# Second batch's scatters spread over heads and logits, joint end chunks, and the token copies moved to ScalarE

## The reference

```python
scores = einsum('bhqd,bhkd->bhqk', q, k) * scale
sparsity = scores.max(-1) - scores.mean(-1)
_, top_idx = top_k(sparsity, U)                      # U = 307 of 2048
out_sel = softmax(q_sel @ k.T * scale) @ v
out = zeros_like(q).at[bi, hi, top_idx].set(out_sel) # a scatter
x = x + ga * (out @ Wo + bo)
logits = einsum('bnd,esd->bnes', xn, sn)             # token x slot
dispatch, combine = softmax(logits, over tokens), softmax(logits, over slots)
slots = einsum('bnd,bnes->besd', xn, dispatch)
eo = gelu(slots @ w1 + b1) @ w2 + b2
x = x + gb * einsum('bmd,bnm->bnd', eo, combine)
```

## Time and profile before

| what | us |
|---|---|
| three timed runs | 1577.94, 1582.79, 1583.1 |
| their median | 1582.79 |
| time of the profiled execution | 1569.39 |
| its span, first to last instruction | 1567.7 |
| attention of batch 0, PE busy from 456 to 580 | 117.70 of 124 |
| attention of batch 1, PE busy from 928 to 1040 | 108.13 of 112 |
| logits of batch 0, PE busy from 1043 to 1100 | 57.00 of 57 |

### The profile page before, as it was taken

The page is one execution under the profiler, slowest core; times in us unless marked ns, Lnnn a source line. Parts: engine busy times, 40 slices in busy tenths (PEclk is TensorE's granted clock), DMA queues, the critical chain, the costliest instruction groups (busy, mean ns, idle before and its releaser), DMA issues.

```text
span 1567.7 us, 28302 instructions
## 1 busy us (share of the span) xinstructions
PE 1457.8 (93%) x8701; PEld 804.4 (51%) x8706; DVE 1203.5 (77%) x2777; ACT 1034.4 (66%) x1420; POOL 270.5 (17%) x331
## 2 busy tenths in 40 slices
PE   7999999998889989999999889999999999999999
PEld 3542222223434432222222644444889986489988
DVE  5679999999887759999999888877855534775411
ACT  4578888887767878888888448863433463343453
POOL 1540000000720042111111214441111000011100
PEclk9999999999999999999999899999999999999999
DMA  5861111112432301111112212220143202024410
GB/s 178 266 170 40 40 40 40 42 44 85 152 106 72 79 12 46 50 48 43 42 42 82 68 38 64 55 75 16 62 162 134 91 33 75 0 85 149 139 48 33
DMA packets 94323, 119.40 MB, mean 76 GB/s; under 512 B 23726, under 2 KB 79630, under 8 KB 93724
## 3 DMA queue, kind: packets, MB, share of 16 engines
q1 hardware_dynamic: 91164, 117.66, 24.8%
q0 software_dynamic: 3072, 0.66, 0.3%
HBM read 93.46 MB, written 24.79 MB: 75 GB/s over the span
## 4 chain that ended last, share of the span: by engine, by line
PE 50%; DVE 34%; issue 11%; DMA 3%; ACT 2%; POOL 1%; SPq 0%; DVEq 0%; ACTq 0%
DVE work_area L1309 26%; PE psum L2156 7%; PE psum L2097 7%; PE psum L2220 7%; PE psum L2016 5%; PE psum L2007 4%; PE psum L2167 4%; PE psum L1988 3%; DVE big_area L1309 3%; PE psum L2176 3%; DMA work_area<-heads_out 2%; PE psum L2210 2%; PE psum L1809 2%; PE psum L1834 1%; DVE work_area L1380 1%
## 5 line engine op out<-in xcount | busy, mean ns | idle before, releaser
L1309 DVE CUSTOM_DVE_ANT_0 work_area<-psum,work_area 128x1024 f32<-128x1024 f32 x512 | 589.1, 1220 | 8.1 <-PE psum L1870 4.3
L902 ACT ACTIVATE work_area<-psum 128x1024 f32<-128x1024 f32 x512 | 510.4, 1027 | 76.2 <-DVE big_area L1309 32.3
L1870 PE MATMUL psum<-work_area 96*128 96x512 bf16 x1024 | 309.4, 384 | 47.9 <-DVE big_area L1309 6.8
L1860 PE MATMUL psum<-work_area 96*128 96x512 bf16 x1024 | 305.4, 380 | 7.4 <-ACT work_area L902 1.6
L1870 PEld LDWEIGHTS psum<-work_area 96*128 96x128 bf16 x1024 | 63.4, 97 | 266.4 <-DVE big_area L1309 251.2
L1860 PEld LDWEIGHTS psum<-work_area 96*128 96x128 bf16 x1024 | 88.7, 98 | 153.0 <-ACT work_area L902 59.0
L924 ACT ACTIVATE work_area<-psum 128x614 f32<-128x614 f32 x160 | 102.3, 682 | 29.8 <-PE psum L2007 28.7
L2156 PE MATMUL psum<-work_area,xn 128*128 128x128 f32 x1024 | 117.4, 275 | 0.5 <-ACT work_area L1008 0.5
L2156 PEld LDWEIGHTS psum<-work_area,xn 128*128 128x128 f32 x1024 | 115.8, 192 | 0.9 <-ACT work_area L1008 0.7
L2220 PE MATMUL psum<-expert_out,work_area 128*128 128x256 f32 x512 | 115.5, 379 | 0.0
L2097 PE MATMUL psum<-slots_T,work_area 128*128 128x512 f32 x256 | 115.0, 592 | 0.0
(11 more groups left out here) (267 smaller groups left out, 2080.4 us busy)
## 6 DMA issues: line engine op xcount, KB each, us to landing
work_area<-in_L_ffn_w_dram SPq DMA_DIRECT2D x32, 1024.0 KB, 5.3
work_area<-k_parts SPq DMA_DIRECT2D x192, 64.2 KB, 2.1
work_area<-q_parts SPq DMA_DIRECT2D x192, 64.0 KB, 2.1
k_parts<-work_area SPq DMA_DIRECT2D x24, 384.0 KB, 3.5
q_parts<-work_area SPq DMA_DIRECT2D x16, 384.0 KB, 2.7
big_area<-q_parts SPq DMA_DIRECT2D x16, 384.0 KB, 5.5
work_area<-k_parts SPq DMA_DIRECT2D x32, 192.0 KB
x_res<-in_L_attn_x_dram SPq DMA_DIRECT2D x8, 512.0 KB, 6.6
```

What stands on the lines that cost most here:

```text
L902: s.activation(SC[:, t % 4], PS[:, 2 * (n % 2):2 * (n % 2) + 2].rearrange("p a n -> p (a n)"), ACT.Relu).then_inc(relu_done, 1)
L1309: v.tensor_tensor_reduce(SC[:, t % 4], PS[:, 4 + 2 * (t % 2):6 + 2 * (t % 2)].rearrange("p a n -> p (a n)"), SC[:, t % 4], 1.0, -3.0e38, A ...
L1860: last = mm(PS[:, 2 * (n % 2) + k], QS1[par][0:TERMS, t * P:(t + 1) * P], KS[par][0:TERMS, k * 512:(k + 1) * 512], start=True, stop=True)
L1870: last = mm(PS[:, 4 + 2 * (t % 2) + k], QS1[par][0:TERMS, t * P:(t + 1) * P], KS[par][0:TERMS, K1 + k * 512:K1 + (k + 1) * 512], start=Tru ...
```

## The change

- `heads_out[b]` gets 16 rows more, one for each head, that nobody reads. The matrix of selected queries `QS` gets 13 more columns, set once for each batch by POOL, whose row number is such a spare row (plus the head).
- The last chunk of an even head stands in partitions 0 to 63 and that of an odd head in partitions 64 to 127 (`chunk_at`), and both share one buffer entry (`ON_ends`, `IDX_ends`), so two heads take 5 scatters and not 6: 40 for a batch. DVE writes each head's rows and places with two instructions each where there was one.
- Both batches keep rows and places of all heads in the space of the first weights. DVE's wait for scatters in `indices` goes; one wait for all scatters of batch 0 stands before the attention of batch 1. SP's and ACT's waits for all scatters before the weights and the slot maxima go too.
- Batch 0's scatters: one in every 6 maxima instead of 5. Batch 1's: the first 26 wait for a number of exponentials, 4.5 apart; the other 14 wait for one turned token tile each of batch 0's logits. `first_rows(1)` still waits for all of them.
- `keep_tokens` moves from POOL to ACT, behind each `turned`.

```diff
-    heads_out = [nc.dram_tensor(f"heads_out{b}", [L * H, DH], F32).ap() for b in range(B)]
+    heads_out = [nc.dram_tensor(f"heads_out{b}", [L * H + H, DH], F32).ap() for b in range(B)]
+    UW = 320
+    chunk_at = lambda j, par: j * P - (HALF_ROWS if j == CH - 1 and par else 0)
+    SCATTERS = (2 * PAIRS, 3 * PAIRS)
+    CHUNKS = [(h, j) for h in range(H) for j in range(CH - 1 + h % 2)]
+    IN_HEADS = 26
...
             def first_rows(b):
                 for k in range(2):
-                    sp.wait_ge(scattered[k], (b + 1) * PAIRS * CH * 16)
+                    sp.wait_ge(scattered[k], (b + 1) * SCATTERS[k] * 16)
...
             def weights(b):
                 sp.wait_ge(oT_used, B * H)
-                for k in range(2):
-                    sp.wait_ge(scattered[k], B * PAIRS * CH * 16)
...
+                for par in range(2):
+                    g.memset(QS[:, par, U:UW], float(L * H // 2))
...
+            def scatter_behind_heads():
+
+                for n, (h, j) in enumerate(CHUNKS):
+                    pool.wait_ge(on_ready, H + h + 1)
+                    if n < IN_HEADS:
+                        pool.wait_ge(p_ready, 2 + 128 + 13 + n * 9 // 2)
+                    else:
+                        pool.wait_ge(xt_ready, n - IN_HEADS + 1)
+                    scatter_one(1, h, j)
...
+                def keep_tokens(i, par, n):
+                    t = i * 2 + n
+                    s.activation(XN[:, t] if isinstance(t, int) else row(XN, t), XS[:, par], ACT.Identity).then_inc(xn_ready, 1)
+
                 if b:
                     turned(b, 0, 0, 0)
+                keep_tokens(0, 0, 0)
                 with act.Fori(0, NT // 2 - 1) as i:
                     for par in range(2):
                         turned(b, i, 1 - par, par + 1)
+                        keep_tokens(i, 1 - par, par + 1)
                         keep_logits(i, par)
...
+                    half = slice(par * HALF_ROWS, (par + 1) * HALF_ROWS)
                     dve.wait_ge(idx_ready, b * H + i * 2 + (n + 1))
-                    if b:
-                        dve.wait_ge(scattered[par], b * (PAIRS * CH * 16) + (i * (CH * 16) + (n // 2) * CH * 16))
-                    v.tensor_scalar(IDX[:, par] if b else of_head(IDX0, i, n), PS[:, 7, CH * P:CH * P + CH], hcol[:, bass.ds(i * 2 + n, 1)], None, ALU.add).then_inc(idx_used, 1)
+                    v.tensor_scalar(of_head(IDX, i, n), PS[:, 7, CH * P:CH * P + CH - 1], hcol[:, bass.ds(i * 2 + n, 1)], None, ALU.add)
+                    v.tensor_scalar(IDX_ends[half, bass.ds(i + n // 2, 1)], PS[half, 7, CH * P + CH - 1:CH * P + CH], hcol[half, bass.ds(i * 2 + n, 1)], None, ALU.add).then_inc(idx_used, 1)
...
-                    v.tensor_tensor(ON[:, par] if b else of_head(ON0, i, n), OR[:, :, 0:DH], ORr.rearrange("p (j o) -> p j o", o=1).to_broadcast([P, CH, DH]), ALU.mult).then_inc(on_ready, 1)
+                    half = slice(par * HALF_ROWS, (par + 1) * HALF_ROWS)
+                    v.tensor_tensor(of_head(ON, i, n), OR[:, 0:CH - 1, 0:DH], ORr[:, 0:CH - 1].rearrange("p (j o) -> p j o", o=1).to_broadcast([P, CH - 1, DH]), ALU.mult)
+                    v.tensor_scalar(ON_ends[half, bass.ds(i + n // 2, 1)].rearrange("p o d -> p (o d)"), OR[half, CH - 1, 0:DH], ORr[half, CH - 1:CH], None, ALU.mult).then_inc(on_ready, 1)
...
+                    for k in range(2):
+                        dve.wait_ge(scattered[k], SCATTERS[k] * 16)
                     spread(0)
```

More of the change, by code:

```diff
@@ L151, in adaln_block @@
         a = Area(Wqk[:].rearrange("p k c n -> p (k c n)"))
-        ON0 = a.take([H, CH, DH])
-        IDX0 = a.take([H, CH], U32)
+        ON = a.take([H, CH - 1, DH])
+        IDX = a.take([H, CH - 1], U32)
+        ON_ends = a.take([PAIRS, DH])
+        IDX_ends = a.take([PAIRS], U32)
         WoG = sb("Wo_gated", [P, DC, D])
@@ L227, in adaln_block @@
         OS = a.take([CH * P])
-        QS = a.take([2, UP], BF16)
+        QS = a.take([2, UW], BF16)
         PX = [a.take([2, UP]) for _ in range(2)]
@@ L235, in adaln_block @@
         ORr = a.take([CH])
-        ON = a.take([2, CH, DH])
-        IDX = a.take([2, CH], U32)
         PX_last = [a.take([2, UP]) for _ in range(2)]
@@ L374, in adaln_block @@
         rowv = lambda v: v.rearrange("(a d) -> a d", a=1).to_broadcast([P, D])
-        heads_rows = [h.rearrange("(t p h) d -> t p (h d)", p=P, h=H) for h in heads_out]
+        heads_rows = [h[0:L * H].rearrange("(t p h) d -> t p (h d)", p=P, h=H) for h in heads_out]
         @block.sync
@@ L426, in zero_rows @@
                 for b in range(B):
[L427 removed]
+                    hz = heads_out[b][0:L * H].rearrange("(p j) d -> p (j d)", p=P)
                     for k in range(2):
@@ L734, in attend, with scatter_chunk @@
[L734 to L752, removed]
+            def scatter_chunk(b, h, j):
+                g.indirect_dma_start(
+                    out=heads_out[b], out_offset=bass.IndirectOffsetOnAxis(ap=IDX[:, h, j:j + 1], axis=0),
+                    in_=ON[:, h, j], in_offset=None).then_inc(scattered[h % 2], 16)
@@ L754, in scatter_in_search, with scatter_ends, scatter_one @@
+            def scatter_ends(b, i):
+                g.indirect_dma_start(
+                    out=heads_out[b], out_offset=bass.IndirectOffsetOnAxis(ap=IDX_ends[:, i:i + 1], axis=0),
+                    in_=ON_ends[:, i], in_offset=None).then_inc(scattered[1], 16)
+            def scatter_one(b, h, j):
+                if j < CH - 1:
+                    scatter_chunk(b, h, j)
+                else:
+                    scatter_ends(b, h // 2)
             def scatter_in_search():
                 pool.wait_ge(zero_out, 64)
[L757 to L763, removed]
+                for n, (h, j) in enumerate(CHUNKS):
+                    pool.wait_ge(max_done, H * NT + 4 + (n + 1) * 6)
+                    scatter_one(0, h, j)
@@ L765, in experts @@
+            def scatter_behind_heads():
+                for n, (h, j) in enumerate(CHUNKS):
+                    pool.wait_ge(on_ready, H + h + 1)
+                    if n < IN_HEADS:
+                        pool.wait_ge(p_ready, 2 + 128 + 13 + n * 9 // 2)
+                    else:
+                        pool.wait_ge(xt_ready, n - IN_HEADS + 1)
+                    scatter_one(1, h, j)
             def experts(b):
-                with pool.Fori(1 - b, NT // 2) as i:
-                    for par in range(2):
-                        keep_tokens(b, i, par)
@@ L814, in _ @@
             pads(1)
-            attend(1)
+            scatter_behind_heads()
             experts(0)
@@ L1000, in slot_maxima @@
                     s.activation(MXR[:, at:end], PS[:, 6:8].rearrange("p a n -> p (a n)")[:, at:end], ACT.Identity).then_inc(mxr_ready, 1)
-                for k in range(2):
-                    act.wait_ge(scattered[k], B * PAIRS * CH * 16)
                 slot_maxima(0, 0, S)
@@ L2022, in rows @@
                     for j in range(CH):
-                        w = min(P, U - j * P)
-                        last = mm(PS[0:w, 7, CH * P + j:CH * P + j + 1], QS[0:TERMS + 5, n % 2, j * P:j * P + w], idx_rows[0:TERMS + 5, 0:1], start=True, stop=True)
+                        at = chunk_at(j, n % 2)
+                        w = min(P, UW - at)
+                        last = mm(PS[0:w, 7, CH * P + j:CH * P + j + 1], QS[0:TERMS + 5, n % 2, at:at + w], idx_rows[0:TERMS + 5, 0:1], start=True, stop=True)
                     last.then_inc(idx_ready, 1)
@@ L2030, in turn @@
                     for j in range(CH):
-                        last = tr(PS[:, 7, j * P:(j + 1) * P], OS[:, j * P:(j + 1) * P], identF[:])
+                        last = tr(PS[:, 7, j * P:(j + 1) * P], OS[:, chunk_at(j, n % 2):chunk_at(j, n % 2) + P], identF[:])
                     last.then_inc(oT_ready, 1)
```

6 lines of the change are left out of this document (1 added, 5 removed).

## The result

| | us, median (range, runs) |
|---|---|
| before, the same session | 1582.47 (1577.94 to 1583.41, 6) |
| after | 1571.88 (1568.75 to 1573.85, 6) |
| ratio | 0.9936, 95% interval 0.9923 to 0.9948 |
| profiled execution, before and after | 1569.39 and 1569.73 |

The changed kernel is 10.6 us faster in timed runs, while the two profiled executions differ by 0.3 us. Forecast was 1582.0 (1574 to 1590), no change. So the trace shown of the kernel before is that of an execution that did not lose the 10 us, and the experiments had to find one that did.

A forecast was written before the change was run, and what follows sets the result against it. The prediction took PE, busy 93% of the span, as the bound. All terms were worth 0 except -0.1 us from the long head, giving 1582.7 for the median of runs; it said 1582, range 1574 to 1590.

The forecast's parts named there:

- Three scatters a head cost a head nothing: In the attentions: heads 7.06 us apart with scatters and without, so scatters do not lengthen a head.
- Scatters of batch 1 out of the attention: Moving batch 1's scatters out of the second attention: worth 0 by the two equal head lengths.
- third rival: In timed runs, 13 us longer than profiled: spreading bursts of scatters gives up to 6.5 us, 1576; chance 0.11.
- The long head: One head of 8.11 us in the second attention: its whole surplus of 1.05 us bounds the gain, 0.1 taken.
- The two DVE instructions: Two more small DVE instructions a head, both attentions: 0.35 us a head, hidden behind DVE's waits, worth 0.
- first rival: In the attentions, DVE's additions reach PE: at most 11.2 us more, 1594; chance 0.09.
- The copies: Token copies on ACT in the logits: 0.42 us each, 1.9 us of ACT's wait remain, worth 0.
- The rows: Batch 1's first rows: issued from 1090.7, landing 1092.9 to 1096.3, before PE asks at 1097.69; worth 0.
- second rival: Batch 1's rows come late after the last scatters: PE waits 0.95 us, 1584; chance 0.07.
- fourth rival: In the logits, DVE and POOL lock each other at 14 scatters: 2.3 us later, 1585; chance 0.05.
- the rule of the Trainium skill: VectorE and GpSimd share an exclusive port lock, so a scatter could hold DVE's maxima 1 us, 2.3 us in sum.

The follow-up runs named there:

- e12: The kernel before, unchanged, in a long session, with a profiled execution that has the loss in it: 1583.06 us, profiled execution 1583.34 us.
- e5: The changed kernel, unchanged, timed beside the kernel before in a short session: 1571.30 us, ratio 0.9998.
- e9: The changed kernel, unchanged, timed again beside the kernel before in a short session: 1571.66 us, ratio 0.9997.
- e14: The changed kernel with batch 1's scatters back in bursts after each pair of heads, in a long session: 1577.95 us, ratio 0.9973 to the kernel before.
- e13: The kernel before without any scatter of the heads' rows, in a long session: 1571.56 us, ratio 0.9938 to the kernel before.
- e10: The changed kernel, unchanged, in a long session: 1571.38 us, ratio 0.9936 to the kernel before.
- e2: The kernel before with only its token copies moved to ACT, in a short session: 1571.88 us, ratio 1.0001 to the kernel before.
- e4: The changed kernel with token copies back on POOL between the spread scatters, in a short session: 1571.40 us, ratio 0.9998 to the kernel before.
- e16: The changed kernel with token copies back on POOL between the spread scatters, in a long session: 1571.53 us, ratio 0.9942 to the kernel before.
- e17: The kernel before with token copies on ACT and its bursts of scatters left, in a long session: 1581.45 us, ratio 1.0000 to the kernel before.
- e6: The kernel before without any indirect DMA, POOL raising the semaphores itself, in a short session: 1571.75 us, ratio 1.0000 to the kernel before.
- e7: The changed kernel with 24 scatters in the heads instead of 26, the last waiting for the 16th turned tile: 1576.02 us, ratio 1.0027 to the kernel before.
- e11: The changed kernel with its last 27 scatters in a row instead of spread, in a long session: 1587.49 us, ratio 1.0022 to the kernel before.
- e15: The changed kernel with 27 scatters in a row from the first turned tile, in a long session: 1592.70 us, ratio 1.0076 to the kernel before.
- e18: The kernel before with batch 1's indirect scatters replaced by plain transfers of the same bytes to fixed rows: 1570.57 us, ratio 0.9936 to the kernel before.

## Why the prediction was wrong

The step that failed is the first of the prediction: "Three scatters a head cost a head nothing", read from equal head lengths, and from it "Scatters of batch 1 out of the attention: [...] worth 0". That holds for the execution that the trace shows. In an execution of a long session they cost 0.87 us a head, 11.2 us in all (e12), and the change takes nearly all of that away. The mechanism is the third rival's, bursts of scatters in the runs, which had a chance of 0.11 and a price of half the unexplained gap. The gap was 13.4 us; 11.2 is the bursts, and the other 2 is that the profiled execution was a short one even for its kind: in short sessions the kernel before took 1568 to 1574 us, 1572 in the median. "Against it: nothing in the trace" was no argument: the trace was of an execution that lay 8.5 us below the shortest timed run, and it could show neither that cost nor its absence. The chance of the rival should have been larger, and its price up to the whole gap. The three timed runs before the change (1577.94 to 1583.1) were of a long session by their times, and so, with 1582.47 us for the kernel before, was the result; in short sessions the change moves nothing, as forecast (e5, e9).

What shares the credit: the change without its spreading gives 4.5 us (e14), where a head in two has two scatters in a row instead of three; spreading them gives the other 6.4 to 6.6 (e14 against e13's 1571.56 in its own session and e10's 1571.38 in another), the copies 0 (e2, e4, e16, e17). The long head, whose surplus of 1.05 us bounded the gain in the prediction, took 8.11 us before, 8.00 after and 7.80 without scatters (e6). The expectation of e12 was wrong in its place too: not the start of the logits, but each head.

The other steps held. The two DVE instructions cost 0.39 us a head (taken: 0.35) and are hidden, against the first rival. The copies cost 0.42 each and left ACT 1.98 us of wait (1.9). The rows were issued at 1091.72, 1 us later than worked out, since the last scatter began at 1089.34, 0.75 us behind the end of the copy that it waits for, and that copy ended 0.3 us later than before; e7 shows that the cover is real and what it costs without (second rival). The fourth rival: no lock is to be seen; DVE is 43.39 us busy in the logits where it was 43.18, beside 14 scatters. On the rule of the Trainium skill (SBUF — State Buffer, Who interferes with whom) the rows stay as they were: even the four maxima of DVE that ran beside the 27 scatters in a row took 1.23 us each in e11.

## What to carry to other kernels

Compare the profiled execution with the timed runs first: where it lies below all of them by more than the runs spread, its trace lacks the cost that matters, and the gap belongs to whatever the change removes until a trace of a long execution says otherwise. Keep GpSimd's indirect DMAs apart where another engine is on the critical path: some 3 to 5 us between their starts took 10 us off here in long sessions and changed nothing in short ones. Where an engine starts late though the releaser named had ended, look at what runs beside it.

## What the runs showed of the hardware

Beside indirect DMAs issued one behind the other ScalarE starts late, and in the heads of the second attention of e12 and e14, but for one small step, no other engine does so first: a head grows by 0.2 us with two in a row (e14) and by 0.9 with three (e12, e14), and beside 27 in a row a tile takes 9.3 to 11.4 us and not 3.65, but only after seven had begun (e15). In the changed kernel, where the first four come in two pairs and the other 36 have 2.7 to 5.0 us between their starts, 11 heads grow by 0.7 us in all, and with plain transfers of the same rows in bursts of three by nothing (e18). The scatters themselves take as long in e12 as in the trace of before (medians 1.03 and 1.03 us).

This stands only in some sessions: the same kernel on the same chip took 1572 and 1582 us, with the same granted clock. The page's bytes and packets of the instruction queues (44 and 43 packets) are the same in e12 as in the trace of before. What sets a session's kind, and by what path ScalarE is held, was not tried and stays open: its own instruction supply and a late signal from PE are both only guesses, and that its input lay ready fits either.

A stall of PE costs more than itself: in e15 PE stood still for 6.09 and 6.02 us, and the eight matmuls after these waits took 5.16 and 6.28 us and not 3.60, at a mean granted clock of 0.71 and 0.58 where it is 1.00 otherwise, so in part at the lower of its two levels (1.2 and 2.4 GHz).
